# Attention outputs normed straight into contiguous rows, and the output bias added one group earlier, in an AdaLN attention and mixture-of-experts layer

## The reference

```python
# x: (4, 1024, 128); 16 heads of 8; 8 experts of width 512, top 2, capacity 1280
mod = (silu(c) @ wmod).reshape(4, 6, 1, 128)      # sa, ca, ga, sb, cb, gb
ga, gb = (sign(g) * max(|g|, 0.25) for g in (ga, gb))
h = layernorm(x) * (1 + ca) + sa
x = x + ga * (causal_attention(h) @ w_out.T + b_out)
h = layernorm(x) * (1 + cb) + sb
x = x + gb * moe(h)     # softmax router, top 2 of 8, capacity-limited dispatch, SwiGLU experts
```

## Time and profile before

| | us |
|---|---|
| median of 3 runs | 956.09 (951.81 to 960.04) |
| the profiled execution: its time | 952.5 |
| its span, first to last instruction | 950.5 |
| mean granted TensorE clock, share of full | 0.841 |

### The profile page before, as it was taken

The page is one execution under the profiler, slowest core; times in us unless marked ns, Lnnn a source line. Parts: engine busy times, 40 slices in busy tenths (PEclk is TensorE's granted clock), DMA queues, the critical chain, the costliest instruction groups (busy, mean ns, idle before and its releaser), DMA issues.

```text
span 950.5 us, 17156 instructions
## 1 busy us (share of the span) xinstructions
PE 728.3 (77%) x5876; PEld 397.3 (42%) x5876; DVE 566.9 (60%) x1066; ACT 460.4 (48%) x903; POOL 394.3 (41%) x432
## 2 busy tenths in 40 slices
PE   4655688889979798879787979886208999999950
PEld 2332233333324223324222333222207888888850
DVE  6859588888677876777866687511603333333314
ACT  2540467777656555656554556562003444444420
POOL 5541111113152164152155153155360777777762
PEclk9975599999789977989977799765557999999985
DMA  4244723551101111101111000000023554543237
GB/s 122 76 158 158 153 66 67 97 113 36 35 2 36 35 37 47 36 2 35 35 33 49 2 2 2 2 26 21 0 62 90 89 90 90 89 87 38 26 28 182
DMA packets 68177, 55.97 MB, mean 59 GB/s; under 512 B 7040, under 2 KB 58752, under 8 KB 68096
## 3 DMA queue, kind: packets, MB, share of 16 engines
q1 hardware_dynamic: 54528, 45.40, 18.4%
q0 software_dynamic: 13568, 9.51, 7.3%
HBM read 29.19 MB, written 25.31 MB: 57 GB/s over the span
## 4 chain that ended last, share of the span: by engine, by line
PE 59%; DVE 12%; issue 8%; ACT 8%; DMA 6%; POOL 4%; SPq 2%; DVEq 0%; ACTq 0%; POOLq 0%
PE psum L858 15%; PE psum L843 13%; PE psum L1058 11%; PE psum L1082 8%; ACT prob_all L1200 7%; PE psum L818 4%; DVE mx L1392 3%; DMA k_parts<-prob_all 2%; POOL slot_rows L626 2%; PE psum L867 2%; PE psum L826 1%; DVE xn L1333 1%; DMA slot_rows<-early,idxb 1%; SPq L366 1%; PE psum L880 1%
## 5 line engine op out<-in xcount | busy, mean ns | idle before, releaser
L1200 ACT ACTIVATE prob_all<-psum 128x512 f32<-128x512 f32 x576 | 318.0, 598 | 219.2 <-PE psum L843 207.7
L1392 DVE TENSOR_REDUCE mx<-psum 128x2 f32<-128x1024 f32 (+3 forms) x384 | 347.2, 953 | 117.9 <-PE psum L818 57.5
L843 PE MATMUL psum<-stack 51*128 51x512 bf16 (+3 forms) x768 | 199.2, 365 | 64.5 <-ACT prob_all L1200 44.3
L641 POOL TENSOR_SCALAR_AFFINE_SELECT prob_all<-prob_all 128x512 f32<-128x512 f32 x128 | 79.0, 635 | 358.9 <-ACT prob_all L1200 351.8
L858 PE MATMUL psum<-prob_all,vst 128*32 128x512 f32 (+3 forms) x1536 | 181.8, 575 | 3.1 <-POOL prob_all L641 3.1
L818 PE MATMUL psum<-stack 48*128 48x512 bf16 (+3 forms) x768 | 164.9, 370 | 19.8 <-DVE mx L1392 11.7
L736 POOL DMA_INDIRECT sums<-ys,dest_of x80 | 124.6, 1558 | 81.0 <-ACT ys L1262 53.4
L843 PEld LDWEIGHTS psum<-stack 51*128 51x128 bf16 x768 | 49.4, 96 | 236.0 <-ACT prob_all L1200 165.9
L1758 DVE TENSOR_TENSOR hid<-psum,hT 128x512 f32<-128x512 f32 (+1 forms) x96 | 57.1, 602 | 94.1 <-ACT hT L1255 66.4
L626 POOL DMA_INDIRECT slot_rows<-early,idxb x64 | 62.8, 981 | 41.8 <-issue 18.4
L826 PE MATMUL psum<-mask_k,mask_q 64*128 64x64 bf16 x1024 | 75.6, 200 | 0.0
(11 more groups left out here) (178 smaller groups left out, 687.8 us busy)
## 6 DMA issues: line engine op xcount, KB each, us to landing
slot_rows<-fill SPq DMA_DIRECT2D x4, 1300.0 KB, 11.4
vals<-slot_rows SPq DMA_DIRECT2D x8, 650.0 KB
stack<-q_parts SPq DMA_DIRECT2D x32, 96.0 KB
stack<-k_parts SPq DMA_DIRECT2D x32, 96.0 KB
xs<-x SPq DMA_DIRECT2D x4, 512.0 KB, 6.4
stack<-q_parts SPq DMA_DIRECT2D x32, 64.0 KB
stack<-k_parts SPq DMA_DIRECT2D x32, 64.0 KB
early<-w1T SPq DMA_DIRECT2D x8, 256.0 KB
```

The costliest lines, as they stand in the source:

```text
L641: ins = nc.gpsimd.affine_select(out=v, in_=v, compare_op=ALU.is_ge, fill=0.0, base=0, pattern=[[0, GH], [1, P]], channel_multiplier=-1)
L843: mm = nc.tensor.matmul(psum[:, KB[s % 2], col:col + w], kst[buf][r, hp, kb * P:kb * P + P], qst[buf][r, hp, qc * 512 + q0:qc * 512 + q0 + ...
L1200: nc.scalar.activation(probs[kind % NP][:, h, :], psum[:, KB[s % 2], :], ACT.Exp, scale=SCALE).then_inc(exped, 1)
L1392: ins = nc.vector.tensor_reduce(mx[:, part, :, hp, i], psum[:, QB[u % 2]:QB[u % 2] + 2, col:col + w], AX.X, ALU.max)
```

## The change

`ys` becomes a plain tile of 2,560 columns, and `yc` its first 1,024 columns, as two halves of `[128, 4 tokens, 128]`. `normed` writes a group's 32 columns of each token straight into `yc`, at the offset 32 m, which is now a constant of the program. The POOL copies and their semaphore `y_cont` go; `turn_y` waits for `o_norm` in their place. Because `yc` is written again by the next batch, two `normed` of each batch from 1 on (that of group 0 at step 24 and that of group 1 at step 11) first wait for `turn_y` of the batch before (`yT_mm`). The bias additions (`add_bias`) stand in the batch's own group 3, behind the masks of kind 2 and ahead of the scatters, for all four batches; the two additions behind the last group go. As `ys` is 6 KB per partition smaller, the tiles declared after it lie at lower addresses, and `yc` no longer shares memory with `xn`.

```diff
--- before.py
+++ after.py
@@ -124,7 +124,7 @@
 
         xs = sb("xs", [P, NT, D])
         vals = sb("vals", [P, NN, BT, 32])
-        ys = sb("ys", [P, NN, BT, 32])
+        ys = sb("ys", [P, 2 * CAP])
         modrow = sb("modrow", [P, NB, 4, D])
         rT_s = sb("rT_s", [P, NE])
         wo_s = sb("wo_s", [P, D])
@@ -174,7 +174,8 @@
         mv2 = [sb(f"mv2{i}", [P, 4, 2]) for i in range(2)]
         vpe2 = [sb(f"vpe2{i}", [P, 4]) for i in range(2)]
         rstd2 = [sb(f"rstd2{i}", [P, 4]) for i in range(2)]
-        yc, yT = xn, hT
+        yc = [ys[:, i * 512:i * 512 + 512].rearrange("p (t d) -> p t d", t=4) for i in range(2)]
+        yT = hT
         h2T = [xn[i][:].rearrange("p t d -> p (t d)") for i in range(2)]
         rows = early[:, 3072:3072 + 2 * BT * ROW].rearrange("p (k t r) -> p k t r", k=2, t=BT)
         dests = sb("dests", [P, 2, NT], I32)
@@ -243,7 +244,7 @@
         w_h, w_l = ([sb(f"w_{n}{i}", [P, 2 * F], F32R) for i in range(2)] for n in "hl")
         x_h, x_l = ([sb(f"x_{n}{i}", [P, CAP], F32R) for i in range(2)] for n in "hl")
         flat_vals = vals[:].rearrange("p n t d -> p (n t d)")
-        flat_ys = ys[:].rearrange("p n t d -> p (n t d)")
+        flat_ys = ys[:]
         NX = ST * ROW
         xr = [flat_vals[:, i * NX:(i + 1) * NX].rearrange("p (s r) -> p s r", s=ST) for i in range(2)]
         yo = [flat_ys[:, i * CAP:(i + 1) * CAP].rearrange("p (s d) -> p s d", s=ST) for i in range(2)]
@@ -283,8 +284,8 @@
 
         pool_waited, act_waited, dve_waited = sem("pool_waited"), sem("act_waited"), sem("dve_waited")
 
-        gates_folded, y_cont, yT_mm, yT_ready, proj_mm, bias_in, x1_ready = (
-            sem(n) for n in ("gates_folded", "y_cont", "yT_mm", "yT_ready", "proj_mm", "bias_in", "x1_ready"))
+        gates_folded, yT_mm, yT_ready, proj_mm, bias_in, x1_ready = (
+            sem(n) for n in ("gates_folded", "yT_mm", "yT_ready", "proj_mm", "bias_in", "x1_ready"))
         n2_stats, n2_aggr, n2_step, rstd2_ready, h2_step, h2_ready, h2_kept, h2T_mm, h2T_ready = (
             sem(n) for n in ("n2_stats", "n2_aggr", "n2_step", "rstd2_ready", "h2_step", "h2_ready", "h2_kept",
                              "h2T_mm", "h2T_ready"))
@@ -557,15 +558,8 @@
             pool.wait_ge(gates_folded, 2 * NB)
             pool.wait_ge(dest_ready, 2)
 
-            def gather_heads(b):
-
-                pool.wait_ge(o_norm, b * (2 * NG) + 2 * NG)
-                pool.sem_inc(pool_waited, 1)
-                for half in range(2):
-                    nc.gpsimd.tensor_copy(
-                        yc[half][:].rearrange("p t (g d) -> p t g d", g=NG),
-                        ys[:, bass.ds(b * NG, NG), 4 * half:4 * half + 4, :].rearrange("p g t d -> p t g d")
-                    ).then_inc(y_cont, 1)
+            def add_bias(b):
+
                 for half in range(2):
                     xv = xs[:, bass.ds(b * BT + 4 * half, 4), :]
                     nc.gpsimd.tensor_tensor(xv, xv, gab[:, bass.ds(b, 1), :].to_broadcast([P, 4, D]),
@@ -647,8 +641,8 @@
                             after(pool, pv_done, n * NK)
                             pool.sem_inc(pool_waited, 1)
                             stage_v(n + 1, (m + 1) % 2)
-                        if mix and m == 0:
-                            gather_heads(b - 1)
+                        if m == 3:
+                            add_bias(b)
                         if mix and m == 1:
                             for half in range(2):
                                 second_norm(b - 1, half)
@@ -676,16 +670,6 @@
             for m in range(NG):
                 group(NB - 1, m, m == NG - 1, True)
 
-            b = NB - 1
-            for half in range(2):
-                xv = xs[:, b * BT + 4 * half:b * BT + 4 * half + 4, :]
-                nc.gpsimd.tensor_tensor(xv, xv, gab[:, b:b + 1, :].to_broadcast([P, 4, D]), ALU.add).then_inc(bias_in, 1)
-            for half in range(2):
-                pool.wait_ge(o_norm, 2 * NN - 1 + half)
-                nc.gpsimd.tensor_copy(
-                    yc[half][:].rearrange("p t (g d) -> p t g d", g=NG),
-                    ys[:, b * NG:b * NG + NG, 4 * half:4 * half + 4, :].rearrange("p g t d -> p t g d")
-                ).then_inc(y_cont, 1)
             row_dests(NB - 1)
             for half in range(2):
                 second_deviation(NB - 1, half)
@@ -869,7 +853,7 @@
 
             def turn_y(b, half, bank):
 
-                pe.wait_ge(y_cont, b * 2 + half + 1)
+                pe.wait_ge(o_norm, (b + 1) * (2 * NG) - 1 + half)
                 for i in range(4):
                     mm = nc.tensor.transpose(psum[:, bank, i * P:i * P + P], yc[half][:, i, :], identf[:])
                 mm.then_inc(yT_mm, 1)
@@ -1414,14 +1398,14 @@
                 dve.wait_ge(m_step, k + 4)
                 nc.vector.tensor_tensor(low, res, mid, ALU.subtract).then_inc(m_step, 1)
 
-            def normed(count, n, chunk):
+            def normed(count, m, chunk):
 
                 dve.wait_ge(oT_mm, count)
                 o = psum[:, MISC, :].rearrange("p (t h d) -> p t h d", t=4, h=GH)
                 nc.vector.reciprocal(rec[:].unsqueeze(3), o[:, :, :, HD:HD + 1]).then_inc(o_rec, 1)
                 dve.wait_ge(o_rec, count)
                 nc.vector.tensor_tensor(
-                    ys[:, bass.ds(n, 1), 4 * chunk:4 * chunk + 4, :].rearrange("p n t (h d) -> p (n t) h d", h=GH),
+                    yc[chunk][:, :, 32 * m:32 * m + 32].rearrange("p t (h d) -> p t h d", h=GH),
                     o[:, :, :, 0:HD], rec[:].unsqueeze(3).to_broadcast([P, 4, GH, HD]),
                     ALU.mult).then_inc(o_norm, 1)
 
@@ -1561,9 +1545,13 @@
                     if mix and m == 3 and s == 6:
                         ranks(p, MISC)
                     if s == 11 and not first:
-                        normed(n * 2, n - 1, 1)
+                        if mix and m == 1:
+                            dve.wait_ge(yT_mm, p * 2 + 2)
+                        normed(n * 2, (m - 1) % NG, 1)
                     if s == 24:
-                        normed(n * 2 + 1, n, 0)
+                        if mix and m == 0:
+                            dve.wait_ge(yT_mm, p * 2 + 1)
+                        normed(n * 2 + 1, m, 0)
                     if mix and m == 1 and s in (4, 16):
                         add_attention(p, s // 16, MISC)
                     if mix and m == 1 and s in (6, 18):
@@ -1595,7 +1583,7 @@
                     group(b, m, False, 2, True)
             for m in range(NG):
                 group(NB - 1, m, False, min(2, NG - 1 - m), True)
-            normed(NN * 2, NN - 1, 1)
+            normed(NN * 2, NG - 1, 1)
 
 
             b = NB - 1
```

## The result

The changed kernel takes 961.55 us (median of 13 runs, 956.73 to 966.53), the kernel before 952.01 (13 runs beside it, 948.44 to 960.04). The ratio is 1.0087, 95% interval 1.0062 to 1.0113: 0.9% slower, where I had forecast 0.4% faster, and outside my range. The profiled execution took 966.53 us with a span of 964.8, against 952.5 with 950.5; the mean granted clock is 0.826 instead of 0.841. It is the slowest of the 13: its rows lose 14.3 us of span where the medians differ by 9.5.

What follows compares the result with a forecast made beforehand. It took a chain of waits as the bound: mostly PE in attention groups, a single thread behind the last. Terms 3.63 + 0.5 gave 4.1 us less, 956.09 to 952.0 us; range 946 to 959.

Steps and rivals of the forecast that it cites:

- The tail, 3.63: Behind the last group, PE's transposes of `yc` wait for DVE's `normed` alone and start 3.63 us earlier.
- The additions moved, priced at 0: In the fourth groups, POOL's pauses before the mask of kind 7 absorb the 2.48 us of additions: 0.
- New waits, priced at 0: DVE's two `normed` waits for `yT_mm` in batches 1 to 3 never hold: 0, at most 0.4 us.
- `normed` without a register: In the loops, DVE's gap from reciprocal to multiplication falls from 0.18 to 0.04 us: 0.5 us less, up to 2.2.
- The copies in the groups, 0: Dropping POOL's copies inside the groups gains nothing, because PE's own earlier work covers them: 0.
- Addresses, 0: Tiles after `ys` move down by 6 KB, and no row depends on an address: 0.
- Rival "POOL is late": In fourth groups, pauses fail to absorb the additions, masks slip and PE's `values` waits: 3.3 us slower, 959.4; chance 0.08.
- Rival "the clock comes back in the tail": In the tail, PE's 16 projection matmuls run at the upper clock: 1.8 us more off, 950.2; chance 0.12.
- Rival "stalls at loop ends move": PE's unexplained 3.65 us stall at the first pass's end vanishes or comes twice: 948.3 or 955.6 us; chance 0.10.
- Rival "DVE and POOL block each other": Six additions in batches 1 to 3 each hold a DVE instruction 1.24 us: 7.4 back, 959.4 us; chance 0.04.

Runs made afterwards that it cites:

- f1: The changed kernel as it is, measured again on chip 9: 962.69 us against 954.35 for the kernel before, ratio 1.0113.
- f4: The changed kernel with the additions behind the fourth group's mask of kind 0, ahead of masks 1 and 2: 951.75 us against 954.35, ratio 0.9967.
- h1: The changed kernel with DVE's two waits in place but on a prologue signal instead of `yT_mm`; ratio to the kernel before between 1.0061 and 1.0086.
- g2: The changed kernel without DVE's two waits for `yT_mm` per batch, on chip 5: 944.99 us against 950.81 for the kernel before, ratio 0.9961.
- f2: The changed kernel with `ys` at its old size and `y_cont` still allocated, so old addresses and semaphores: 963.71 us, ratio 1.0101.

## Why the prediction was wrong, point by point

- **The tail, 3.63**: right. Measured 3.71 between two fixed points of the traces, and the releaser is DVE's `normed`, as forecast.
- **The additions moved, priced at 0**: this is the step that failed. Its own argument held. The pauses took up the delay, and PE's waits for POOL ahead of `values` are those of before:

```profile
L842 PE MATMUL psum<-prob_all,vst 128*32 128x512 f32 (+3 forms) x1536 | 186.4, 587 | 3.5 <-POOL prob_all L635 3.4
```

  3.4 us, against 3.1 before. I looked only at who waits for POOL, and here two engines were held up that do not: ACT and DVE waited for signals of PE. Priced at 0, additions in front of the scatters cost 10.9 us, f1's 962.69 against 951.75 for f4, which has them behind the mask of kind 0, on the same chip. In the first pair of traces the three stretches grow by 15.3 us (6.6, 5.0 and 3.7 by batch), in an execution that is 5 us above its median. Why later scatters go with late signals of PE stays open.
- **New waits, priced at 0**: they never hold. If they have a part in the loss, it is not through what they wait for (h1). g2 has neither them nor the loss, but ran on a chip without late releases; so whether the sum lacks a term for the waits and the delay together is not shown.
- **`normed` without a register**: the gap is what I said, 0.03 instead of 0.18:

```profile
357.51 0.25 DVE L1405 RECIPROCAL rec<-psum 128x16 f32<-128x16 f32 x1
357.79 0.29 DVE L1407 TENSOR_TENSOR ys<-psum,rec 128x128 f32<-128x128 f32 x1
```

  Whether that is worth 0.5 us no run separates.
- **The copies in the groups, 0**: nothing in the groups shows a gain from them. **Addresses, 0**: not the loss (1.0101 in f2 beside 1.0113 in f1).
- **Rival "POOL is late"**: not what happened; that it gave the nearest time (959.4) is luck. POOL waits for ACT behind the run (5.50 us), not the other way round.
- **Rival "the clock comes back in the tail"**: no. The 16 matmuls of the projection take 406 ns each, against 401 before.

```profile
L864 PE MATMUL psum<-wog,hT 128*128 128x128 f32 x16 | 3.5, 406 | 0.0
```

- **Rival "stalls at loop ends move"**: the stall of rows 11 is there as before, a little longer:

```profile
371.10 0.60 PE L827 MATMUL psum<-stack 51*128 51x512 bf16 x1 [4.07 <-issue]
```

  It was the nearest in kind, a stall with no cause in the rows that comes with a change of the programs, but I looked for it in one place, once, at 3.65 us and a chance of 0.10. It came three times, in the fourth groups, on other engines, and with a loss of clock.
- **Rival "DVE and POOL block each other"**: no. A pair of maxima beside the additions takes 2.35 to 2.36 us, as in the same group before (2.36 at 333.46, 2.35 at 336.33):

```profile
337.33 2.36 DVE L1376 TENSOR_REDUCE mx<-psum 128x2 f32<-128x1024 f32 x2
...
340.09 2.35 DVE L1376 TENSOR_REDUCE mx<-psum 128x2 f32<-128x1024 f32 x2
```

  By the Trainium skill, "SBUF — State Buffer", section "Who interferes with whom", they could not collide, since the maxima read PSUM; the trace agrees.

The range, 946 to 959, was too narrow at its upper end: it let a stall of the kind of rows 11 come once, and did not price the clock behind it. The tail's gain came true and was outweighed.

## What to carry to other kernels

Moving work in front of a run of indirect DMAs can cost engines that wait for neither: price it not only by who waits for the issuing engine, and try the work well ahead of the run (f4). Where a gain and a harmless move come in one change, as here, build them apart: the tail's gain needed neither the move nor its place. Price a stall of PE with the clock that it may lose: here a release 3.1 us late went with 6.6 us, another 2.7 us late with 4.3. And run the slow kernel itself beside its variants on every chip: a variant without the stall says nothing on a chip on which nothing stalls.

## What the runs showed of the hardware

In the changed kernel's trace PE's signals to ACT and DVE are recorded some 3 us behind the modelled ends of their matmuls (3.12 and 2.93 in the first stall), three times in its fourth groups, during or shortly after scatters of 0.97 us issued 0.30 apart. The same kind of wait stands at the end of the second loop pass in the traces of both kernels and in all eight from chips 9 and 8 (3.1 to 3.8 us of idle ACT), and nowhere in the eight from chips 12 and 5. PE's mean granted clock was 0.93 over the 4 us in which the first of these stalls lies and 0.51 over the 10 us behind it; without the stall it was 0.80 over 4 us at the same step and 1.00 over the 8 us behind.
